# GNN layer on one core: source rows by column copies for two tiles in 32 instead of one, 32 columns per step and engine, and one function table on ScalarE

## What is computed

```python
msg_in = concatenate([nodes[row], nodes[col], edge_features], axis=-1)
messages = relu(msg_in @ mW1 + mb1) @ mW2 + mb2
aggregated = segment_sum(messages, col, num_segments=nodes.shape[0])
upd = relu(concatenate([nodes, aggregated], axis=-1) @ uW1 + ub1) @ uW2 + ub2
x = layernorm(x + upd)          # row = src, col = dst
```

## Time and profile before

| | us |
|---|---|
| median of 3 runs | 2066.56 (2063.19 to 2068.11) |
| the profiled execution | 2065.72 |
| its span, first to last instruction | 2063.9 |
| POOL busy | 1523.9 (74%) |
| PE busy | 1375.5 (67%) |
| DVE busy | 1202.1 (58%) |
| ACT busy | 855.5 (41%) |

### The profile page before, as it was taken

How to read it: one execution, slowest core, us unless ns; L and a number is a source line. 1 busy time by engine, 2 the same in 40 slices (tenths; PEclk the granted TensorE clock), 3 DMA queues, 4 the chain that set the end, 5 groups by cost and what they waited for, 6 DMA issues and landing times.

```text
span 2063.9 us, 44951 instructions
## 1 busy us (share of the span) xinstructions
PE 1375.5 (67%) x8520; PEld 1297.1 (63%) x8520; DVE 1202.1 (58%) x4540; ACT 855.5 (41%) x4449; POOL 1523.9 (74%) x1625
## 2 busy tenths in 40 slices
PE   6667567766766656777667666666666767656667
PEld 5666556756665656766556666655666656656666
DVE  5547566566566566566566566566566565566563
ACT  3234344444444444444444344444444444444441
POOL 7737777777777777777777777777777777777774
PEclk8789777687778888767887877888788877888786
DMA  9534444444443443444444344443343443444341
GB/s 233 162 98 133 106 121 108 110 120 108 112 119 108 109 121 108 117 113 110 113 115 112 112 114 108 111 119 108 108 122 108 119 111 108 110 120 110 106 108 38
DMA packets 137562, 237.18 MB, mean 115 GB/s; under 512 B 58948, under 2 KB 84387, under 8 KB 137081
## 3 DMA queue, kind: packets, MB, share of 16 engines
q1 hardware_dynamic: 77728, 127.22, 21.4%
q0 software_dynamic: 51552, 104.05, 20.1%
q10 hardware_dynamic: 8254, 5.59, 1.2%
HBM read 227.11 MB, written 9.60 MB: 115 GB/s over the span
## 4 chain that ended last, share of the span: by engine, by line
POOL 65%; issue 24%; PE 3%; DMA 2%; ACT 1%; SPq 1%; POOLq 1%; DVE 1%; DVEq 1%; ACTq 0%
POOL gath L662 65%; DMA table_src<-gath 1%; DMA gath<-table_src,idx 1%; PE ps_sum L794 1%; PE ps_pre L769 1%; PE ps_pre L770 1%; DMA col_src<-in_srcT_dram 0%; PE ps_pre L735 0%; SPq L501 0%; PE ps_pre L776 0%; DMA xwin<-in_xT_dram 0%; DVE col_x L445 0%; POOLq L656 0%; ACTq L902 0%; DVEq L442 0%
## 5 line engine op out<-in xcount | busy, mean ns | idle before, releaser
L662 POOL DMA_INDIRECT gath<-table_src,idx x1488 | 1404.5, 944 | 454.0 <-issue 450.5
L776 PE MATMUL ps_pre<-rhs,lhs 128*128 128x128 f32 x3226 | 606.8, 365 | 643.1 <-DVE lhs L1084 640.4
L776 PEld LDWEIGHTS ps_pre<-rhs,lhs 128*128 128x128 f32 x3226 | 560.7, 270 | 673.7 <-issue 363.2
L1105 DVE TENSOR_TENSOR hid<-ps_pre,gath 128x1024 f32<-128x1024 f32 x203 | 247.2, 1218 | 640.6 <-DMA gath<-table_src,idx 608.9
L445 ACT COPY col_x<-xdeg 64x1 f32 x3624 | 378.0, 191 | 234.0 <-issue 234.0
L794 PE MATMUL ps_sum<-onehot,hid 128*128 128x96 f32 x3322 | 453.0, 295 | 3.9 <-ACT hid L948 2.3
L794 PEld LDWEIGHTS ps_sum<-onehot,hid 128*128 128x128 f32 x3322 | 442.8, 213 | 13.2 <-ACT hid L948 3.0
L948 ACT ACTIVATE hid<-hid 128x1024 f32<-128x1024 f32 x203 | 213.3, 1051 | 505.5 <-DVE hid L1105 505.0
L445 DVE COPY col_x<-xdeg 64x1 f32 x2818 | 326.9, 144 | 152.0 <-issue 148.5
L1084 DVE TENSOR_SCALAR_CACHE_REDUCE lhs<-lhs,place 96x1024 f32<-96x1024 int32 x208 | 262.8, 1263 | 23.2 <-PE ps_sum L710 11.7
L1076 DVE TENSOR_TENSOR onehot<-ps_iota,dst_rel 128x768 f32<-128x768 f32 (+1 forms) x209 | 197.5, 945 | 0.1
(11 more groups left out here) (106 smaller groups left out, 753.8 us busy)
## 6 DMA issues: line engine op xcount, KB each, us to landing
lhs<-in_dst_dram SPq DMA_DIRECT2D x207, 384.0 KB
lhs<-in_edgeT_dram SPq DMA_DIRECT2D x207, 128.0 KB, 2.4
gath<-table_src,idx POOLq DMA_INDIRECT x1488
table_src<-gath SPq DMA_DIRECT2D x12, 512.0 KB, 8.2
xwin<-in_xT_dram SPq DMA_DIRECT2D x208, 24.0 KB
xrow<-in_x_dram SPq DMA_DIRECT2D x48, 64.0 KB
out_dram<-yout ACTq DMA_DIRECT2D x48, 64.0 KB, 1.7
xdeg<-in_xT_dram ACTq DMA_DIRECT2D x4, 512.0 KB, 10.4
```

The lines of the kernel that those rows point to most:

```text
L662: pool.indirect_dma_start(gath[0:m, k, j * H:(j + 1) * H], None, table_src, src_by_tile(p, k, j, m)).then_inc(to, 16)
L776: mm = nc.tensor.matmul(to[0:m, j * H:(j + 1) * H], lhs[:, k, j * P:j * P + m], rhs[:, k, :], start=True, stop=not by_cols)
L1105: nc.vector.tensor_tensor(hid[0:m, k, at], ps_pre[k % 2][0:m, at], gath[0:m, k, at], ALU.add).then_inc(hsum_made, 1)
```

## The change

Tile 7 is now made from columns in two slots of four, 1 and 3 (`COL_K = (1, 3)`), for iterations from COL_FIRST = 3 on (pair 13 is the first). Each has its own list, `col_x` and semaphores. Every step now has copies, on ACT columns 0 to 63 and on DVE 64 to 127, in halves of 32: slot 1 at k = 1 and 2 of the iteration before, slot 3 at k = 3 of the one before and at k = 0. SP asks for the lists at k = 0 and k = 2. Four iterations are written out on every engine instead of two (POOL: three). ACT computes one Sqrt at its start, so that the table set that is loaded first holds all of its functions.

```diff
-COL_K = SLOTS - 1
+PEELED = 4
+COL_K = (1, 3)
+COL_FIRST = 3
 COL_TILE = PT - 1
-COL_STEPS = 3
-COLS_ACT, COLS_DVE = 24, 18
-COLS_DVE_LAST = P - COL_STEPS * COLS_ACT - (COL_STEPS - 1) * COLS_DVE
+COL_HALF = P // 4
...
-            at, part = (it + 1, 0) if k == COL_K else (it, k + 1)
-            return (at, part) if part < COL_STEPS and not (isinstance(at, int) and not 0 < at < ITERS - 1) else None
+            at = it if k == 0 else it + 1
+            return None if isinstance(at, int) and not COL_FIRST <= at < ITERS - (k == 0) else (at, 1 - k % 2)
...
+            at, half = cols_for(it, k)
+            i = 1 if k in (0, 3) else 0
+            eng.wait_ge(col_src_in[i], (at - COL_FIRST + 1) * 16)
+            if half == 0 and not (isinstance(at, int) and at == COL_FIRST):
+                eng.wait_ge(pe_steps, steps_for_pre((at - 1) * SLOTS + COL_K[i]))
             let(eng)
-            eng.load(regs[0:count], col_src[0:1, at:at + count])
-            for i in range(count):
+            start = first + half * COL_HALF
+            eng.load(regs, col_src[0:1, i, start:start + COL_HALF])
+            for n in range(COL_HALF):
...
-                if k == COL_K and not (isinstance(it, int) and it == ITERS - 1):
+                if k in (0, 2) and not (isinstance(it, int) and not COL_FIRST <= it + 1 < ITERS):
...
                 for j, m in tiles_of(p):
-                    if j == COL_TILE and has_cols(p, k):
+                    if j == COL_TILE and has_cols(it, k):
                         break
...
-            act.wait_ge(consts, 1)
+            act.wait_ge(consts, 7)
+            nc.scalar.activation(root[:, :], eps[:, :], ACT.Sqrt)
...
-                    copy_cols(act, nc.scalar.copy, col_regs, *cols_for(it, k), False, cols_act)
+                    copy_cols(act, nc.scalar.copy, col_regs, it, k, 0, cols_act)
...
-                    copy_cols(dve, nc.vector.tensor_copy, col_regs, *cols_for(it, k), True, cols_dve)
+                    copy_cols(dve, nc.vector.tensor_copy, col_regs, it, k, 2 * COL_HALF, cols_dve)
```

More of the change, by code:

```diff
@@ L240, in gnn_kernel @@
         rhs_made = sem("rhs_made")
-        col_src_in = sem("col_src_in")
-        cols_act = sem("cols_act")
-        cols_dve = sem("cols_dve")
+        col_src_in = [sem(f"col_src_in{i}") for i in range(len(COL_K))]
+        cols_act = [sem(f"cols_act{i}") for i in range(len(COL_K))]
+        cols_dve = [sem(f"cols_dve{i}") for i in range(len(COL_K))]
         col_zero = sem("col_zero")
@@ L345, in steps_for_window, with pairs @@
             return p - 2
-        def pairs(eng, step, node, tail, peeled=2):
+        def pairs(eng, step, node, tail, peeled=PEELED):
             for it in range(peeled):
@@ L431, in copy_cols @@
[L431 to L440, removed]
-            let(eng)
-            eng.load(regs[0:count], col_src[0:1, at:at + count])
-            for i in range(count):
-                src = eng.snap(regs[i], min_val=0, max_val=N - 1)
-                ins = copy(col_x[:, at + i:at + i + 1], xdeg[0:D, bass.ds(src, 1)])
-            ins.then_inc(done, 1)
+            if k in COL_K and not (isinstance(it, int) and it < COL_FIRST):
+                return (it - COL_FIRST) * (16 * COL_TILE) + (COL_FIRST - first) * (16 * PT) + 16 * t
@@ new lines, in got, with has_cols, cols_done, copy_cols @@
+            return (it - first) * (16 * PT) + 16 * t
+        def has_cols(it, k):
+            return k in COL_K and not (isinstance(it, int) and (it < COL_FIRST or (it, k) == (ITERS - 1, COL_K[1])))
+        def cols_for(it, k):
+            at = it if k == 0 else it + 1
+            return None if isinstance(at, int) and not COL_FIRST <= at < ITERS - (k == 0) else (at, 1 - k % 2)
+        def cols_done(it):
+            return (it - COL_FIRST + 1) * 2
+        def copy_cols(eng, copy, regs, it, k, first, done):
+            at, half = cols_for(it, k)
[3 more added lines that the diff above has]
+                eng.wait_ge(pe_steps, steps_for_pre((at - 1) * SLOTS + COL_K[i]))
+            let(eng)
+            start = first + half * COL_HALF
+            eng.load(regs, col_src[0:1, i, start:start + COL_HALF])
+            for n in range(COL_HALF):
+                src = eng.snap(regs[n], min_val=0, max_val=N - 1)
+                ins = copy(col_x[:, i, start + n:start + n + 1], xdeg[0:D, bass.ds(src, 1)])
+            ins.then_inc(done[i], 1)
@@ L559, in step @@
                     load_pair(*pair(it, k, -PREP))
-                if k == COL_K and not (isinstance(it, int) and it == ITERS - 1):
[L561 to L564, removed]
+                if k in (0, 2) and not (isinstance(it, int) and not COL_FIRST <= it + 1 < ITERS):
+                    i = k // 2
+                    if not (isinstance(it, int) and it + 1 == COL_FIRST):
+                        sp.wait_ge(cols_act[i], cols_done(it))
+                        sp.wait_ge(cols_dve[i], cols_done(it))
+                    of = srcT[:, cols((it + 1) * (SLOTS * PT) + COL_K[i] * PT + COL_TILE, 1)].rearrange("p a -> a p")
+                    sp.dma_start(col_src[:, i, :], of, allow_slow_non_contiguous=True).then_inc(col_src_in[i], 16)
             def node(c, k, m, i=0):
@@ L665, in _ @@
                 pool.wait_ge(idx_rest_in, 16)
-                pairs(pool, step, lambda *chunk: None, lambda i: None, peeled=3)
+                pairs(pool, step, lambda *chunk: None, lambda i: None)
             with pool.Else():
@@ L774, in pre @@
                 for j, m in tiles_of(p):
-                    by_cols = j == COL_TILE and has_cols(p, k)
+                    by_cols = j == COL_TILE and has_cols(it, k)
                     mm = nc.tensor.matmul(to[0:m, j * H:(j + 1) * H], lhs[:, k, j * P:j * P + m], rhs[:, k, :], start=True,
@@ L778, in pre @@
                     if by_cols:
-                        pe.wait_ge(cols_act, it * COL_STEPS)
-                        pe.wait_ge(cols_dve, it * COL_STEPS)
-                        mm = nc.tensor.matmul(to[:, j * H:(j + 1) * H], col_x[:, :], w_src[0:D, :], start=False, stop=True)
+                        i = COL_K.index(k)
+                        pe.wait_ge(cols_act[i], cols_done(it))
+                        pe.wait_ge(cols_dve[i], cols_done(it))
+                        mm = nc.tensor.matmul(to[:, j * H:(j + 1) * H], col_x[:, i, :], w_src[0:D, :], start=False, stop=True)
                 return mm
@@ L932, in _ @@
             fit = act.value_load(fits[0:1, 0:1], min_val=0, max_val=1)
-            col_regs = [act.alloc_register(f"act_col{i}") for i in range(COLS_ACT)]
+            col_regs = [act.alloc_register(f"act_col{i}") for i in range(COL_HALF)]
             def relu_raw(p):
@@ L1099, in add_gathered @@
                 dve.wait_ge(pe_steps, steps_for_pre(p))
-                by_cols = has_cols(p, k)
+                by_cols = has_cols(it, k)
                 dve.wait_ge(gathered_tail, 16) if part else dve.wait_ge(gathered[k], got(it, k, COL_TILE if by_cols else t))
-                if by_cols and isinstance(it, int) and it == 1:
-                    dve.wait_ge(col_zero, 1)
+                if by_cols and isinstance(it, int) and it == COL_FIRST:
+                    dve.wait_ge(col_zero, len(COL_K))
                 at = slice(first * H, (first + t) * H)
@@ L1107, in _ @@
             ends = {}
-            col_regs = [dve.alloc_register(f"dve_col{i}") for i in range(max(COLS_DVE, COLS_DVE_LAST))]
+            col_regs = [dve.alloc_register(f"dve_col{i}") for i in range(COL_HALF)]
             def copy_idx(p, it, k):
@@ L1135, in step @@
                 ahead = pair(it, k, 1 - SLOTS)
-                if ahead and not (isinstance(it, int) and (ahead[0] < 3 * SLOTS or it == ITERS - 1)):
+                if ahead and not (isinstance(it, int) and (ahead[0] < PEELED * SLOTS or it == ITERS - 1)):
                     copy_idx(*ahead)
@@ L1144, in step @@
                     add_sums(*pair(it, k, 3))
-                if isinstance(it, int) and (it, k) == (1, 1):
-                    dve.wait_ge(rows_stored[0][COL_K], 16 * sum(q % SLOTS == COL_K for q, _ in TABLE))
-                    nc.vector.memset(gath[:, COL_K, COL_TILE * H:PW], 0.0).then_inc(col_zero, 1)
+                if isinstance(it, int) and (it, k) == (COL_FIRST, 0):
+                    dve.wait_ge(hsum_made, COL_FIRST * SLOTS)
+                    for i in COL_K:
+                        nc.vector.memset(gath[:, i, COL_TILE * H:PW], 0.0).then_inc(col_zero, 1)
                 if cols_for(it, k):
-                    copy_cols(dve, nc.vector.tensor_copy, col_regs, *cols_for(it, k), True, cols_dve)
+                    copy_cols(dve, nc.vector.tensor_copy, col_regs, it, k, 2 * COL_HALF, cols_dve)
             def tail(i):
```

16 lines of the change are left out of this document (5 added, 11 removed).

## The result

| | before | changed kernel |
|---|---|---|
| median, us | 2066.56 (2063.19 to 2068.11, 5 runs) | 2053.01 (2048.25 to 2054.63, 5 runs) |
| profiled execution, us | 2065.72 | 2048.25 |
| its span, us | 2063.9 | 2046.3 |
| POOL busy, us | 1523.9 | 1479.4 |
| DVE busy, us | 1202.1 | 1648.8 |

The ratio is 0.9932, 95% interval 0.9912 to 0.9952. The kernel became faster, by 0.7% and not by the 4.0% that were forecast, and the time lies outside the predicted range. Between the two profiled executions 17.5 us were gained where 81.0 had been expected; 63.5 us are missing.

What follows compares the result with a forecast made beforehand. POOL's gathers were taken as the bound, 92% of the span. 2065.7 − 58.7 (fewer gathers) − 22.3 (later first columns), with copies, table loads and the rest at 0, gave 1984.7 us, 4.0% less; range 1976 to 2010.

Steps and rivals of the forecast that it cites:

- the one on code: DVE's longer loop body: if fetched anew each iteration, stops add 0.35 us a step, giving 8.85, below POOL's 9.37.
- Rival 4: DVE or ACT only just the bound through many small slips: steps of 9.4 to 9.7 us, 1985 to 2045 us; chance 0.06.
- 1516 gathers at a pitch of 1.25 us: POOL's gathers: 47 fewer, 1516 in all, at 1.2487 us each, saving 58.7 us if POOL stays the bound.
- The start: Before the loops: first columns made later, so POOL's early stalls shrink; gain 22.3 us, bounds 0 and 24.3.
- Rival 1: Start gives nothing back, since PE and loads delay it: 2005.8 us; with what lies between, 1992 to 2007, chance 0.10.
- The register loads: Loads of 32 registers before the column copies: 2.0 us taken, bounds 1.7 to 7.2 us.
- rival 2: DVE's 32-register load runs at the slow rate: 2210 us at 4.06 us a load, over 2800 at 7.2; chance 0.06.
- Rival 3: DVE's copies hold up POOL for 144 ns each: 498 us more, 2480 us; chance 0.02.
- Without their removal ACT's squares and the next ReLU would no longer fit: ACT's CENTER step: table loads, 2.6 us an iteration, must go for work to fit behind the copies; cost and gain 0.

Runs made afterwards that it cites:

- experiment 1: Changed kernel with 45 semaphore increments on DVE ahead of its loops, so its loop body lies over three code blocks, not four: 1983.12 us, ratio 0.9603.
- Experiment 4: Changed kernel with columns in slot 3 alone (one tile of four), none at k = 1 and 2, 1565 gathers: 2045.41 us, ratio 0.9904.
- experiment 5: Sqrt at ACT's start removed from the changed kernel: 2054.80 us; removed from experiment 1's kernel: 1985.29 us; added alone to the kernel before: 2067.59 us.
- 68 more: Changed kernel with 68 semaphore increments on DVE ahead of its loops, body at 31 to 391, over four blocks: 2099.41 us, ratio 1.0161.

## Why the prediction was wrong

**The step that failed** is the one on code: "If all of it is fetched anew each time, three to four such stops an iteration add 0.35 us a step: 8.85, still below 9.37." That it would be fetched anew was seen; the price was taken from the only row at hand, a stop between two instructions that follow one another, where the next block is fetched ahead. Behind the branch back no packet is under way (the first starts 1.9 us later). It costs 3.9 us, eleven times as much, and comes on top of the three stops. Per turn: 34.3 us of DVE's own work (34.0 forecast) + 3.9 + 1.0 = 39.2, above POOL's 37.46. With that term at its measured size the rest of the working would have given the new bound, DVE at 39.2 a turn against 38.73 before, but not the time: 2065.7 − 22.3 + 44 × 0.48 = 2064.6 us, about the kernel before. That the profiled execution came out lower, at 2048.25, is due to the end, which is 18.3 us shorter because POOL runs ahead; the prediction had no term for it. Rival 4 had the right engine and the right kind of cause, "many small slips", at 0.06; there was one large one, and a step of 39.2/4 = 9.8 us lies just above the 9.4 to 9.7 that it allowed.

The Trainium skill, Runtime: NRT & Kernel Launch, section Instruction fetch mechanics, was right in kind where I set it aside: a taken branch to a page that is no longer held stalls. Its two pages are of 256 instructions each; the traces here show blocks of 128, and that a body over three of them stays and one over four does not. There the measurement decides.

**What held.**
- 1516 gathers at a pitch of 1.25 us. In experiment 1 the sum comes out: 1983.1 against 1984.7.
- The start, −22.3. In the changed kernel ReLU of pair 5 ran at 104.28 (forecast 104.5) and the gathers of pair 10 began at 107.39 (107.6). Experiment 4 gives 22.4 us for it. Rival 1 falls.
- The register loads, 2.0 us for 32. Rows of the line of the loads, min/median/max in ns:

```profile
L442 ACTq TENSOR_LOAD <-col_src x195: 1942/1962/1987, 119.2 to 2002.2; - x195
L442 DVEq TENSOR_LOAD <-col_src x195: 2095/2101/2174, 119.2 to 2000.0; - x195
```

All 390 are at the fast rate, so rival 2 falls. That the start column decides it is still only argued: no run of the changed kernel had another.
- No hold-up of POOL by DVE's copies: with 128 a turn instead of 56 the gathers of experiment 1 keep their pitch, 37.39/30 = 1.246 us. Rival 3 falls. The lock that the Trainium skill, SBUF — State Buffer, section SBUF: two separate sides, describes between VectorE and GpSimd was not seen for copies of one column.

**What else was wrong.** "Without their removal ACT's squares and the next ReLU would no longer fit" is refuted by experiment 5: with both table loads in the turn, 1985.29 against 1983.12, with ratios whose intervals overlap. ACT had more room than its chain of longest pieces suggested. It changed nothing in the sum, which had it at 0.

**The bound on the unknown cost** was the fault behind the fault. The price of a branch back to code that must be fetched stands in no row of before, and the prediction gave it no range, only the value of a row for something else. The range should have asked at what price of the branch DVE becomes the bound: (9.37 − 8.85) × 4 = 2.1 us a turn.

## What to carry to other kernels

Before a hardware loop on a tightly timed engine grows, count the instructions of one turn and where its body starts in the blocks of that engine's code; the packets on the instruction queue tell at once whether it is fetched in every turn, and an unexplained "issue" ahead of the first instruction of a body is what it looks like on the timeline. A few cheap instructions ahead of the loop can move it into one block fewer, and should be tried before a change is called a failure. And a slack on which a sum rests must be held against the price of what is not in the trace, not only against what is.

## What the runs showed of the hardware

- Code of DVE and ACT comes in blocks of 128 instructions. A body that touches three is fetched once; over four it is fetched in every turn: (253 − 33)/44 = 5.0 packets a turn, the four and one more. A body of 360 instructions can be either. By the times of the packets the fifth is the block behind the loop, read ahead when the fourth is entered (0.7 us behind that edge in the changed kernel, and between branch and body with 68 more). That it pushes out the first, as with a store of four blocks, would fit all of this; it is argued, and no run shows the size of the store by itself.
- Behind the branch that costs 3.6 (ACT), 3.9 and 4.9 us (DVE); at a block's edge in straight code 0.34.
- For one and the same work the place of the loop alone gave 1983, 2053 and 2099 us, from 4.0% faster than before to 1.6% slower. On the slower chip it was 2921 and 3045 us.
- An engine that falls back does not show at once: POOL kept its full rate for the first 700 us, until its lead was spent. A look at the start of the run alone would have missed the new bound.
